# A scan layer with attention woven in: attention products moved from GpSimd to VectorE, operands kept in PSUM, and two update steps fused

## The reference

```
x = x + A(layernorm(x))   # selective scan: 8 heads, head size 64, state size 128, over the 512 steps
x = x + F(layernorm(x))   # ternary-weight projection 128 -> 128 with bias
x = x + B(layernorm(x))   # attention, 16 heads of 8, over the FIRST axis (8 sequences), at each of the 512 steps
x = x + F(layernorm(x))   # the same projection again
```

```
qkv = x @ in_proj_w.T + in_proj_b                       # q, k, v: (8, 512, 128)
attn = softmax(q·k / sqrt(8)) ; out = attn·v ; out @ out_proj_w.T + out_proj_b
```

## Time and profile before

| | |
|---|---|
| Median of 3 runs | 717.43 us (717.13 to 723.93) |
| The profiled execution's own time | 722.47 us |
| Its span | 720.7 us |
| Mean granted TensorE clock | 0.901 |
| PE busy | 565.0 us, 78% |
| DVE busy | 532.6 us, 74%, 1006 instructions |
| ACT busy | 432.8 us, 60% |
| POOL busy | 531.2 us, 74%, 568 instructions |

### The profile page before, as it was taken

One profiled execution on the slowest core, in us unless ns is written; L12 is line 12 of the kernel. 1 busy time (PEld: TensorE's weight loads), 2 busy tenths in 40 slices (PEclk: granted clock), 3 DMA queues, 4 the chain that ended last, 5 costly groups with the idle time before them and its releaser, 6 DMA issues.

```text
span 720.7 us, 13131 instructions
## 1 busy us (share of the span) xinstructions
PE 565.0 (78%) x3872; PEld 455.1 (63%) x3872; DVE 532.6 (74%) x1006; ACT 432.8 (60%) x1244; POOL 531.2 (74%) x568
## 2 busy tenths in 40 slices
PE   4867999979996668969996668988986579686155
PEld 4746888857874556857875557876765467452144
DVE  6475878777759998765759998776679996621873
ACT  4446888877785454866775454878865348533002
POOL 5506999987769899867769898878678996321881
PEclk8887999999999889998999889999997879967569
DMA  9431132312111101222111101222211011000000
GB/s 204 141 93 53 57 92 58 105 51 65 49 50 50 50 1 49 84 66 64 51 50 49 50 2 49 86 74 77 71 50 25 26 50 46 27 3 0 1 0 29
DMA packets 53343, 39.59 MB, mean 55 GB/s; under 512 B 8339, under 2 KB 49046, under 8 KB 53270
## 3 DMA queue, kind: packets, MB, share of 16 engines
q1 hardware_dynamic: 44822, 34.51, 16.3%
q10 hardware_dynamic: 8448, 4.20, 2.0%
HBM read 33.44 MB, written 4.46 MB: 53 GB/s over the span
## 4 chain that ended last, share of the span: by engine, by line
PE 39%; POOL 22%; DVE 15%; issue 15%; ACT 7%; DMA 1%; POOLq 0%; ACTq 0%; DVEq 0%; SPq 0%
PE ps L1161 7%; POOL area L360 5%; PE ps L1315 4%; PE ps L1283 4%; PE ps L1382 4%; PE ps L1296 3%; ACT area L750 3%; DVE area L1052 2%; PE ps L1325 2%; POOL area L355 2%; POOL bn L518 2%; PE ps L1235 2%; PE ps L1372 2%; PE ps L1237 2%; PE ps L1236 2%
## 5 line engine op out<-in xcount | busy, mean ns | idle before, releaser
L713 ACT ACTIVATE turned<-ps,sct 128x128 f32<-128x128 f32 x512 | 139.4, 396 | 1.8 <-PE ps L1237 0.7
L960 DVE TENSOR_TENSOR_SCAN lmat<-arow,band 128x512 f32<-128x512 f32 x64 | 104.4, 1631 | 3.5 <-POOL band L536 2.3
L517 POOL TENSOR_TENSOR bn<-turned 128x256 f32<-128x256 f32 x64 | 62.2, 972 | 58.1 <-ACT turned L700 41.2
L700 ACT ACTIVATE turned<-ps,sct 128x128 f32<-128x128 f32 x256 | 72.9, 370 | 42.0 <-DVE turned L946 41.6
L1283 PE MATMUL ps<-cT,bT 128*128 128x128 f32 x512 | 76.6, 297 | 21.5 <-issue 12.9
L1283 PEld LDWEIGHTS ps<-cT,bT 128*128 128x128 f32 x512 | 69.0, 208 | 33.1 <-issue 32.2
L536 POOL TENSOR_TENSOR band<-bandm,sct 128x512 f32<-128x512 f32 x64 | 73.8, 1153 | 19.5 <-DMA sct<-packed 19.5
L355 POOL TENSOR_TENSOR area<-area 128x1024 f32<-128x1024 f32 x21 | 59.3, 2840 | 16.5 <-ACT area L618 13.3
L360 POOL TENSOR_TENSOR area<-area 128x1024 f32<-128x1024 f32 x28 | 70.7, 2546 | 0.6 <-DVE area L1056 0.6
L517 POOL TENSOR_TENSOR cn<-turned 128x256 f32<-128x256 f32 x64 | 49.0, 766 | 29.8 <-ACT turned L713 29.4
L618 ACT ACTIVATE area<-ps 128x256 f32<-128x256 f32 (+2 forms) x96 | 41.1, 480 | 46.2 <-PE ps L1161 31.6
(11 more groups left out here) (183 smaller groups left out, 1446.2 us busy)
## 6 DMA issues: line engine op xcount, KB each, us to landing
arow<-alpha_rows SPq DMA_DIRECT2D x32, 512.0 KB, 4.2
drow<-decay_rows SPq DMA_DIRECT2D x64, 128.0 KB, 3.1
area<-in_L_attn_a_x_dram SPq DMA_DIRECT2D x4, 512.0 KB, 6.1
xT_rows<-turned SPq DMA_DIRECT2D x4, 512.0 KB, 3.7
xt<-xT_rows SPq DMA_DIRECT2D x32, 64.0 KB, 2.5
area<-in_L_attn_a_x_dram ACTq DMA_DIRECT2D x8, 256.0 KB, 2.8
out_dram<-area ACTq DMA_DIRECT2D x8, 256.0 KB, 2.3
area<-L_attn_a_sel_proj_w_dram SPq DMA_DIRECT2D x2, 512.0 KB, 6.4
```

Source lines behind the costliest of these rows:

```text
L517: pool.tensor_tensor(out[:, 0], zc[:, 0], zs[:, 1], ALU.subtract)
L713: last = act.activation(dst[h][:, N * q:N * q + N], bank(BK_C)[:, N * q:N * q + N], ACT.Copy, scale=sct[i2][:, at + HH * h + q:at + HH * h ...
L960: dve.tensor_tensor_scan(lmat[h], arow[i2][:, HH * P * h:HH * P * (h + 1)], band[h], 0.0, ALU.mult, ALU.add).then_inc(l_dve, 1)
```

## The change

- Attention products run all on DVE; POOL has none. Product and reduction keep their places.
- Queries are projected by a piece of their own (`f_query`, one per half: four sequences of 128 columns) and stay in the half's PSUM bank, from which the product reads them. Keys and values are projected in pairs of sequences (`f_kv`: two of 256 columns) and copied to SBUF by ACT, two instructions for a pair.
- The exponential is written by ACT into the same PSUM bank, and products 8 to 15 and the sums read it there.
- The state update becomes four fused instructions, one a head: `state = state*decay + own`, all after the wait for PE.
- The first residual step becomes four fused instructions of 128 columns, with the constant moved into the weights `w_out`.
- The bias rows are laid out again (12 small DMAs for 9).
- The second pair of keys and values, and the queries, wait for ACT's copy of the pair before, in the tail too.

The diff, cut to its core:

```diff
-USES = [[("T", g), ("F", g), ("T", 2 + g)] + [("Q", 4 * g + s) for s in range(4)] +
-        [("T", 4 + g), ("O", g), ("T", 6 + g), ("F", 2 + g)] for g in range(2)]
+USES = [[("T", g), ("F", g), ("T", 2 + g), ("KV", 2 * g), ("KV", 2 * g + 1), ("Q", g),
+         ("T", 4 + g), ("O", g), ("T", 6 + g), ("F", 2 + g)] for g in range(2)]
...
-POOL_PRODUCTS = (1, 2, 5, 6, 7, 8, 9, 10, 12, 13, 14, 15)
-LAST_POOL_PRODUCTS = (1, 2, 4, 5, 6, 7, 8, 9, 10, 11, 12, 13, 14)
...
-         "addF0": 47.02, "load:1": 48, "var1:0": 48.01, "rs1:0": 50, "xn1:0": 50.01, "T2": 51, "qkv0": 52,
-         "qadd0": 52.01, "rr:1": 52.02, "qkv1": 53, "x1:1": 53.01, "qadd1": 54, "var0:1": 54.01, "qkv2": 55,
-         "rs0:1": 56, "xn0:1": 56.01, "T1": 57, "F1": 58, "addF1": 58.01, "qadd2": 59, "var1:1": 59.01, "rs1:1": 60,
-         "qkv3": 61, "xn1:1": 61.01, "T3": 62, "qkv4": 63, "qadd4": 63.01, "qkv5": 64, "qadd5": 64.01, "qadd3": 65,
-         "qkv6": 65.01, "qadd6": 65.02, "qkv7": 66, "qadd7": 67, "prod0": 67.01, "prod1": 67.02, "red0": 68,
+         "addF0": 47.02, "load:1": 48, "var1:0": 48.01, "rs1:0": 50, "xn1:0": 50.01, "T2": 51, "KV0": 52,
+         "kvout0": 52.01, "rr:1": 52.02, "KV1": 53, "x1:1": 53.01, "kvout1": 54, "var0:1": 54.01, "Q0": 61.02,
+         "rs0:1": 56, "xn0:1": 56.01, "T1": 57, "F1": 58, "addF1": 58.01, "var1:1": 59.01, "rs1:1": 60,
+         "xn1:1": 61.01, "T3": 62, "KV2": 63, "kvout2": 63.01, "KV3": 64, "kvout3": 64.01, "Q1": 66,
+         "prod0": 67.01, "prod1": 67.02, "red0": 68,
...
+            def f_kv_out(c, q):
+
                 after(act, f_red, 2 * NB * c)
+                act.wait_ge(f_pe[q // 2], use_done(("KV", q), c))
+                rows = f_bank(("KV", q), c).rearrange("p (s e) -> p s e", s=2)
+                evac(ks[:, 2 * q:2 * q + 2, :], rows[:, :, 0:D])
+                evac(vals[:, :, 2 * q:2 * q + 2].rearrange("p e s -> p s e"), rows[:, :, D:2 * D]).then_inc(f_q[q // 2], 1)
...
-                act.activation(rows, rows, ACT.Exp, scale=float(AD) ** -0.5).then_inc(f_exp[g], 1)
+                act.activation(q_bank(g), rows, ACT.Exp, scale=float(AD) ** -0.5).then_inc(f_exp[g], 1)
...
-                dec = sct[i2][:, CD + HH * h:CD + HH * h + HH].unsqueeze(2).broadcast_to([P, HH, PD])
-                dve.tensor_tensor(sdec[:].rearrange("p (h q) -> p h q", q=PD), st, dec, ALU.mult).then_inc(sd_dve, 1)
                 dve.wait_ge(s_pe, n + 1)
                 dve.wait_ge(y_pe, n + 1)
-                dve.wait_ge(sd_dve, n + 1)
                 own = bank(BK_G).rearrange("p (h q) -> p h q", q=N)[:, :, 0:PD]
-                dve.tensor_tensor(st, sdec[:].rearrange("p (h q) -> p h q", q=PD), own, ALU.add).then_inc(s_dve, 1)
+                for q in range(HH):
+                    last = dve.scalar_tensor_tensor(st[:, q], st[:, q], sct[i2][:, CD + HH * h + q:CD + HH * h + q + 1], own[:, q],
+                                                    ALU.mult, ALU.add)
+                last.then_inc(s_dve, 1)
...
+                for q in range(4 * g, 4 * g + 4):
+                    last = dve.scalar_tensor_tensor(xres[:, q], oraw[:, q, 0:D], rr_f[:, q:q + 1], xres[:, q], ALU.mult, ALU.add)
+                last.then_inc(f_x[g], 1)
...
             def f_product(c, m):
-                if m not in pool_products(c):
-                    attention_product(dve, c, m, f_prod_v)
+
+                if m >= 2:
+                    dve.wait_ge(f_red, 2 * NB * c + m - 1)
+                if m < NB:
+                    for g in range(2):
+                        dve.wait_ge(f_q[g], 2 * c + 2)
+                    dve.wait_ge(f_pe[m // 4], use_done(("Q", m // 4), c))
+                    dve.tensor_tensor(prod[:, m % 2].rearrange("p (r e) -> p r e", r=NB),
+                                      q_bank(m // 4)[:, D * (m % 4):D * (m % 4) + D].unsqueeze(1).broadcast_to([P, NB, D]), ks,
+                                      ALU.mult).then_inc(f_prod, 1)
+                else:
+                    g, at = (m - NB) // 4, AH * NB * (m % 4)
+                    dve.wait_ge(f_exp[g], c + 1)
+                    weights = q_bank(g)[:, at:at + AH * NB].rearrange("p (h r) -> p h r", r=NB)
+                    dve.tensor_tensor(prod[:, m % 2].rearrange("p (h d r) -> p h d r", r=NB, d=AD),
+                                      weights.unsqueeze(2).broadcast_to([P, AH, AD, NB]),
+                                      vals.rearrange("p (h d) r -> p h d r", d=AD), ALU.mult).then_inc(f_prod, 1)
...
+            def f_kv(c, q):
+
+                f_free(c, ("KV", q))
+                pe.matmul(f_bank(("KV", q), c), ones3[:], bias3[:, BIAS_KV:BIAS_KV + 4 * D], start=True, stop=False)
+                for r in range(2):
+                    last = pe.matmul(f_bank(("KV", q), c)[:, 2 * D * r:2 * D * r + 2 * D], xnT_f[:, 2 * q + r, :], w_qkv[:, D:3 * D],
+                                     start=False, stop=(r == 1))
+                last.then_inc(f_pe[q // 2], 1)
+
+            def f_query(c, g):
+
+                f_free(c, ("Q", g))
+                pe.matmul(q_bank(g), ones3[:], bias3[:, BIAS_Q:BIAS_Q + 4 * D], start=True, stop=False)
+                for r in range(4):
+                    last = pe.matmul(q_bank(g)[:, D * r:D * r + D], xnT_f[:, 4 * g + r, :], w_qkv[:, 0:D], start=False, stop=(r == 3))
+                last.then_inc(f_pe[g], 1)
```

More of the change, by code:

```diff
@@ L133, in x_step @@
     return len(XSTEPS) * c + XSTEPS.index(name) + 1
-def pool_products(c):
-    return LAST_POOL_PRODUCTS if isinstance(c, int) and c == NC - 1 else POOL_PRODUCTS
 def half_of(use):
-    return use[1] // 4 if use[0] == "Q" else use[1] % 2
+    return use[1] // 2 if use[0] == "KV" else use[1] % 2
 def use_done(use, c):
@@ L412, in _ @@
             for k, part in enumerate(bias_parts):
[L413 to L416 removed]
+                for at, src, n in ((BIAS_Q, 0, 1), (BIAS_KV, D, 2), (BIAS_F, 3 * D, 1), (BIAS_O, 4 * D, 1)):
+                    sp.dma_start(bias3[k:k + 1, at:at + 4 * D].rearrange("o (r d) -> o r d", d=n * D),
+                                 part[:, src:src + n * D].unsqueeze(1).broadcast_to([1, 4 // n, n * D])).then_inc(bias_in, 16)
             sp.wait_ge(pa, PA["rows"])
@@ L454, in f_alone @@
         def f_alone(use, c):
-            name = {"T": "T", "F": "F", "O": "O", "Q": "qkv"}[use[0]] + str(use[1])
+            name = use[0] + str(use[1])
             return isinstance(c, int) and c == NC - 1 and PLACE[name] >= POS * UNITS
@@ L581, in _ @@
                     place(pieces, f"rs{k}:{g}", lambda c, k=k, g=g: ln_root(c, k, g))
-            for m in range(2 * NB):
-                place(pieces, f"prod{m}", lambda c, m=m: product(c, m))
             def step(c, k, pieces, first=False, last=False):
@@ L763, in _ @@
                 place(pieces, f"T{t}", lambda c, t=t: f_T_out(c, t))
-            for q in range(NB):
-                place(pieces, f"qadd{q}", lambda c, q=q: f_qkv_out(c, q))
+            for q in range(NB // 2):
+                place(pieces, f"kvout{q}", lambda c, q=q: f_kv_out(c, q))
             def f_load(c, g):
@@ L1039, in f_product @@
             def f_product(c, m):
-                if m not in pool_products(c):
-                    attention_product(dve, c, m, f_prod_v)
-            def f_reduce(c, m):
-                theirs = pool_products(c)
-                if m in theirs:
-                    dve.wait_ge(f_prod_g, len(POOL_PRODUCTS) * c + theirs.index(m) + 1)
-                else:
-                    mine = [q for q in range(2 * NB) if q not in theirs]
-                    dve.wait_ge(f_prod_v, (2 * NB - len(POOL_PRODUCTS)) * c + mine.index(m) + 1)
+                if m >= 2:
[14 more added lines that the diff above has]
+                                      vals.rearrange("p (h d) r -> p h d r", d=AD), ALU.mult).then_inc(f_prod, 1)
+            def f_reduce(c, m):
+                dve.wait_ge(f_prod, 2 * NB * c + m + 1)
                 if m < NB:
@@ L1337, in f_free @@
                     pe.wait_ge(f_T[g], 4 * c + q // 2 + 1)
+                elif what == "KV":
+                    pe.wait_ge(f_q[g], 2 * c + q % 2 + 1)
                 elif what == "Q":
-                    pe.wait_ge(f_q[g], 4 * c + q % 4 + 1)
+                    pe.wait_ge(f_v[g], v_step("onorm", c))
                 else:
@@ L1387, in _ @@
                     place(pieces, f"T{q}", lambda c, q=q: f_turn(c, q))
+                elif what == "KV":
+                    place(pieces, f"KV{q}", lambda c, q=q: f_kv(c, q))
                 elif what == "Q":
-                    place(pieces, f"qkv{q}", lambda c, q=q: f_qkv(c, q))
+                    place(pieces, f"Q{q}", lambda c, q=q: f_query(c, q))
                 else:
```

63 lines of the change are left out of this document (12 added, 51 removed).

## The result

Before: 718.14 us, the median of 4 runs beside the changed kernel (717.13 to 723.93). After: **743.67 us**, the median of 4 runs (741.44 to 746.26). The ratio is 1.034, with a 95% interval of 1.027 to 1.041, so the change costs 24 us (19 to 29); the plain difference of the medians is 25.5. The prediction said 733 and 719 to 744: the median lies 0.3 us inside the upper end. The profiled execution of the changed kernel took 741.44 us, its span 739.7: 19.0 us more than the span of before.

What follows compares the result with a forecast made beforehand. DVE and POOL, both full, were taken to bound the attention stages, DVE alone afterwards. Loop stages +18.5, tail +4.5, keys/values/queries -1.8, residual step and ACT copies -5.5 gave +15.7 us: 733 us from 717.4, range 719 to 744.

Steps and rivals of the forecast that it cites:

- The bound, and the products: Attention stages: DVE-bound after the change; twelve more products a loop stage at 1.13 us each add 13.6 us.
- The rule on the shared read path: A DVE instruction with two SBUF inputs and a GpSimd instruction reading SBUF hold each other off; one PSUM operand escapes.
- The relief: Per loop stage on DVE: scans -3.1 us, DVE's own four products -1.5, state update -1.5 where present.
- Its cover of 0.72: Chunk 0: 0.72 us between state update and PE's next scores, against 0.46 of added wait; costed at nothing outside the stages.
- the sign that PE's scores wait for the state nowhere outside the stages: Expected profile: outside the attention stages, what releases PE's L1283 is not the state update.
- The loop stages: Three attention stages before the tail: 66 us for 60.2 twice, 63.7 for 57.2 in the third; +18.5 us together.
- keep 1, and take the same off for the small operations: Loop stage sum: 1 us of DVE idle time kept of 2.05, and 1 us subtracted for small operations.
- The tail: Tail's attention, all products on DVE: 42.8 us against 38.3, +4.5 us.
- First residual step and ACT's copies: Outside attention: residual step -1.0 us x 8, ACT copies -10 us of ACT time; a third of each counted, together -5.5.
- a third of it counts: Only a third of the time saved on DVE (70% busy) in the residual step was counted: -2.5 us.
- The rival of the residual step at half rate: Fused instructions reading two float32 SBUF tensors run at half rate; residual step 4.4 us more, 736 us; chance 0.04.
- Keys, values and queries in the tail: Before the tail's first product: only two KV groups needed, 7.2 us instead of 9.0, -1.8 us.

Runs made afterwards that it cites:

- e6: The changed kernel with each of the 64 products over half its elements, the other half left out; 704.48 us, ratio to before 0.977.
- e5: The kernel before with all 16 products on DVE, both inputs in SBUF, nothing else changed; 751.37 us, ratio to before 1.043.
- e7: The changed kernel with POOL's old products back, reading ACT's SBUF copies, and the tail's spare transposes before the bank wait; 706.83 us, ratio to before 0.982.
- e3: The changed kernel with the first residual step back in two instructions of 512 columns; 743.20 us, ratio to before 1.033.
- e8: The kernel of e7 with POOL taking every second product (8) instead of 13 in the last chunk; 707.80 us, ratio to before 0.983.

## Why the prediction came out as it did

**The bound, and the products: right.** DVE sets every attention stage (e6). The product from PSUM takes 1.21 us, 1.13 from its start to the next instruction's as I took it, and is never stretched. On the PSUM surcharge of the Trainium skill ("VectorE: DVE Perf Modes", "The TRN2 errata"): the 65 ns don't show; 1209 to 1215 ns from PSUM and reductions that read no PSUM at 1207 and 1208 are alike, so the 4.1 us by that page are not there. The rule on the shared read path ("SBUF — State Buffer", "Who interferes with whom") holds in every run: L1013, L1020 and L963 keep their length beside POOL; L983, the two-input products of e5 and the scans beside POOL's products (2072 ns in e7) do not.

**The relief: right in kind.** Scans 1539 ns for the 1529 forecast. The state update 0.86 us for 0.83 to 0.88. Its cover of 0.72 was read at one unit and taken for all outside the stages; it fails in four of 40, at most 1.8 us that I had put at nothing. So the sign that PE's scores wait for the state nowhere outside the stages did not hold. In the stages it is worth 1.1 to 1.3 us, forecast 1.5.

**The loop stages: too dear.** Forecast +6, +6 and +6.5, measured +4.6, +4.6 and +4.5, so 4.8 us less in three. In the first two, 0.6 each is rounding: 65.6 was summed, and taken as 66 for 60.2, "+6". The rest is in "keep 1, and take the same off for the small operations". DVE's idle time in the stage fell to 0.47 us (64.68 - 64.21), not 1. The small operations gave about the 1 us that was taken off (the softmax steps L1039 and L1051 stand at 692 and 694 ns where they stood at 836 and 925), and DVE's work came out at 64.21 for 64.6. In the third stage the small operations were under-sized: the two subtractions of before took 1710 ns on average and the scaling 994, against 691 for each in after, so these alone gave 2.3 us where 1 was taken off for all. The tail, 42.2 for 42.8, is right within 0.6.

**First residual step and ACT's copies: the term that failed.** I counted -5.5 us and nothing of it is to be seen. I priced four fused instructions at 1.1 us; they take that once (1.14, POOL idle), and 19.6 / 8 = 2.45 on average. The row I priced it from, held a contended time for the old form, and I compared it with an uncontended one for the new. So the step became dearer for DVE, not cheaper (19.6 us against 17.0 in before and 15.6 in e3). Whether "a third of it counts" is right, e3 can't tell: a third of 4.0 us is less than the medians resolve. ACT's copies, -3 of the 5.5, have no experiment of their own. The gaps before stages 1 to 3, where both savings should have shown, came to 0.6 us more in after than in before (412.2 against 411.6), and to the same in the repeat (413.4 both). These gaps wander by more than 1 us between two profiles of one kernel, so a gain of 5.5 should have shown, one of 1 or 2 need not.
The rival of the residual step at half rate is out as to its cause: by its own working the four would take 1.1 + 0.5 = 1.6 us, and with POOL idle they take 1.14. What POOL adds, 19.6 - 8 x 1.1 = 10.8 us, is more than the 4.4 of that rival. The rule of that rival is in the Trainium skill's "Vector Engine (DVE) Microarchitecture Reference", section 7; the trace disagrees.

**Keys, values and queries in the tail: about right.** From the end of the last scores to the first product of the tail it is 38.7 and 40.4 us in the two profiles of after and 41.1 and 40.9 in those of before: 1.4 us less on average, forecast 1.8, with a spread as large.

**The end: missed.** +3 to +3.9 us, because a bank that now lives until the scaling stands behind a wait ahead of the warm-up. I had looked up who reads the bank, but not everything that PE issues behind the wait for it.

**The sum.** +15.7 was forecast. Less 4.8 for the stages, less 0.5 for the tail, plus 5.5 for the gain that didn't come, plus 3 to 3.9 for the end, is 18.9 to 19.8, and the profiled pair differs by 19.0. So the forecast was short by 3 us of the profiled pair and by 8 to 10 of the medians. That the measured median still fell into the range was luck in part: stages priced too high stood against a relief that wasn't there and an end that was missed, and 743.67 is 0.3 us from the edge, beyond which the repeat (744.06) lies.

**What stays open.** The medians say 24 to 25.5 us. Stages, tail and end account for 21.6 in the first pair of profiles and 20.5 in the second; the other 3 or 4 would lie in the gaps, if the stages are as long in the executions that have no profile, and I didn't settle where. One pair of profiles can't show them: the profiled execution of before lies 4.3 us above its kernel's median, that of after 2.2 below. A candidate is the clock: in the first stage it was granted at 0.79 on average for 0.89 (0.82 for 0.91 in the repeat), and PE's projection L1349 then took

```profile
276.62 2.07 PE L1349 MATMUL ps<-w_of,area 128*128 128x128 f32 x8
...
285.78 1.16 PE L1349 MATMUL ps<-w_of,area 128*128 128x128 f32 x8
```

2.07 us at one place and 1.16 at the next, the lower and the upper of TensorE's two clock levels (1.2 and 2.4 GHz). Ahead of the tail's attention, after has four such places in one profile and three in the other, wholly or in part at the lower level, and both profiles of before have none. At 0.9 us a place this would be of the right size for this one line, but what it costs was argued, not isolated.

## What to carry to other kernels

When two engines are both full in a stage, work moved between them costs its whole price on the one and gives back only the contention and the waiting that it took with it: here 13.6 us a stage against 9. Take the cure for the contention (one operand in PSUM) and leave the work spread over both: here 707 us against 744. Price a split instruction by the neighbours it will have, not by its length alone. And when an edit makes a bank live longer, go through all that is issued behind the wait for it, work that was only there to fill time included.

## What the runs showed of the hardware

- A DVE product with one input from PSUM and a POOL product of the same size run fully side by side (1.22 and 2.36 us in e8); where DVE's instructions read two inputs in SBUF, such a POOL product took up to 3.43 us, 2.71 on average over the first stage of before, and DVE's own 1577 ns on average.
- Short POOL instructions hold a 1.22 us DVE product off by only 0.16 us on average (e5), but a group of four 0.35 us instructions by 1.3 us (L983, 2.45 against 1.14). At 177.40 each of the last three is held until 0.15 us behind the end of the POOL instruction beside it: every start met another one.
- Reading a broadcast row or a broadcast, strided pattern from PSUM costs DVE nothing above SBUF: 1215 and 1209 ns for 1024 elements (1215 from SBUF with POOL idle, e5's tail), 681 and 675 for 512.
